# A stack of four graph layers: both score steps of the attention in a row on four banks, new step orders, and another opening

## The reference

```
layer 0: e = leaky((x W1)(x W2)^T), masked by adj; relu(softmax(e) (x W3))
layer 1: h = x W; e_ij = leaky(h_i a1 + h_j a2), masked; elu(softmax(e) h)
layer 2: o1 = relu(x mlp1 + b1)                       (512 hidden channels)
         o2 = elu(elu(GAT without a mask (W_fc, a_fc) of o1)) + o1
         o3 = relu(o2 mlp2 + b2)
         relu(elu(GAT masked by adj (W_hand, a_hand) of o3) + o3)
layer 3: attention with 4 heads of 64 channels: q, k, v with biases,
         softmax(q k^T / 8, masked) v, then wo and bo
```

## Time and profile before

| | |
|---|---|
| median of 3 runs | 2618.84 us (2617.55 to 2623.7) |
| the profiled execution | 2616.98 us, span 2615.2 us |
| mean granted TensorE clock | 0.988 |
| TensorE busy | 2525.4 us, 97% of the span, 21399 products |
| VectorE busy | 2251.1 us, 86% |
| ScalarE busy | 1968.4 us, 75% |
| GpSimd busy | 1913.2 us, 73% |
| bytes moved by DMA | 329.67 MB, 126 GB/s |

### The profile page before, as it was taken

How to read it: one execution, slowest core, us unless ns; L and a number is a source line. 1 busy time by engine, 2 the same in 40 slices (tenths; PEclk the granted TensorE clock), 3 DMA queues, 4 the chain that set the end, 5 groups by cost and what they waited for, 6 DMA issues and landing times. The chain is left out here.

```text
span 2615.2 us, 64667 instructions
## 1 busy us (share of the span) xinstructions
PE 2525.4 (97%) x21399; PEld 2411.0 (92%) x21399; DVE 2251.1 (86%) x6252; ACT 1968.4 (75%) x4737; POOL 1913.2 (73%) x2439
## 2 busy tenths in 40 slices
PE   6899999999999999999999999999999999999886
PEld 5789999999999999999999999999999999999874
DVE  2478999899999998999999999999989999998874
ACT  2468877887887788778778877877887788787652
POOL 2457877877787877778787777878777787877543
PEclk8899999999999999999999999999999999999998
DMA  4214444444444444444444444344444444443333
GB/s 141 67 52 128 129 142 130 126 139 130 136 123 145 127 126 142 129 138 121 145 126 130 139 134 133 124 142 128 131 134 136 132 128 141 128 132 110 105 106 89
DMA packets 317115, 329.67 MB, mean 126 GB/s; under 512 B 35313, under 2 KB 248689, under 8 KB 316785
## 3 DMA queue, kind: packets, MB, share of 16 engines
q1 hardware_dynamic: 316784, 325.54, 41.5%
HBM read 174.41 MB, written 150.99 MB: 124 GB/s over the span
## 5 line engine op out<-in xcount | busy, mean ns | idle before, releaser
L1234 POOL TENSOR_TENSOR p<-p,rd 128x512 f32<-128x512 f32 x256 | 343.1, 1350 | 5.5
L1159 POOL TENSOR_TENSOR proT_lo<-sco,proT_hi 128x512 fp32r<-128x512 f32 x128 | 165.8, 1295 | 159.7 <-ACT proT_hi L560 159.7
L1171 POOL TENSOR_SCALAR xn<-act,nmean,rstd 128x256 f32<-128x256 f32 x384 | 237.1, 627 | 47.7 <-DVE act L1075 35.3
L786 ACT ACTIVATE p<-p,nmx 128x256 f32<-128x256 f32 x512 | 253.0, 496 | 10.9 <-DVE nmx L1109 10.9
L573 ACT ACTIVATE sco<-sco,nmax 128x256 f32<-128x256 f32 x384 | 192.6, 502 | 40.9 <-DVE nmax L872 36.1
L1181 POOL TENSOR_TENSOR act<-act,x 128x512 f32<-128x512 f32 x64 | 82.9, 1295 | 167.8 <-ACT act L623 167.8
L1109 DVE CUSTOM_DVE_ANT_0 p<-ps,mask 128x256 f32<-128x256 f32 x512 | 188.3, 414 | 15.4 <-PE ps L510 14.0
L872 DVE CUSTOM_DVE_ANT_0 sco<-ps,mask 128x256 f32<-128x256 f32 x384 | 144.9, 414 | 53.2 <-ACT ps L563 41.2
L808 DVE TENSOR_TENSOR xnT_lo<-ps,xnT_hi 128x512 fp32r<-128x512 f32 x192 | 129.7, 675 | 61.0 <-ACT xnT_hi L560 61.0
L1166 POOL TENSOR_TENSOR rstd<-vare,mhalf 128x2 f32<-128x2 f32 x256 | 178.1, 696 | 0.0
L1124 DVE STREAM_TRANSPOSE p<-p 128x1024 f32<-128x1024 f32 x128 | 158.6, 1239 | 18.0 <-POOL p L1234 17.7
(11 more groups left out here) (240 smaller groups left out, 12396.6 us busy)
## 6 DMA issues: line engine op xcount, KB each, us to landing
scratch<-p SPq DMA_DIRECT2D x128, 512.0 KB, 3.0
p4T<-scratch SPq DMA_DIRECT2D x512, 128.0 KB, 3.5
scratch_pro<-act SPq DMA_DIRECT2D x192, 256.0 KB, 2.3
sco<-scratch_pro SPq DMA_DIRECT2D x768, 64.0 KB, 1.9
x0Tp<-in_xT SPq DMA_DIRECT2D x64, 256.0 KB, 2.6
x<-in_x SPq DMA_DIRECT2D x64, 256.0 KB, 2.8
scratch_o<-sco SPq DMA_DIRECT2D x64, 256.0 KB, 2.1
o3r<-scratch_o SPq DMA_DIRECT2D x256, 64.0 KB, 2.5
```

The costliest lines, as they stand in the source:

```text
L786: ins = nc.scalar.activation(rows_, rows_, ACT.Exp, scale=-1.0, bias=nmx4[:, h, m:m + 1], accum_out=den4[:, h, m:m + 1])
L1159: return G.tensor_tensor(lo, whole, hi.bitcast(fp32), ALU.subtract)
L1171: ins = G.tensor_scalar(xn[:, m, :], y[:, m, :], nmean[i][:, m:m + 1], rstd[i][:, m:m + 1], ALU.add, ALU.mult)
L1234: G.tensor_tensor(rows_, rows_, rd4[:, h, :].unsqueeze(2).unsqueeze(3).broadcast_to([P, NT, QUADS, CT * QP]), ALU.mult).then_inc(S["p4n"], 1)
```

## The change

- **Scores.** s40 keeps banks 7 and 6, s42 goes to banks 0 and 1 (`SCORE_BANKS`). On TensorE s40 and s42 follow each other directly, and v2 and w2 come behind them instead of between.
- **Orders.** All five lists are new. Most engines keep the sequence in the main and start the list at another place (which raises or lowers a stage by one for the steps that pass the seam). Besides the scores: on TensorE x0 moves from beside f3 to just ahead of s40, and f1 behind h0; on ScalarE g0 and a few others move, and t0 stands ahead of n2 where t1 stood; on VectorE e0 and t0 come earlier, k4 and v4 later; on GpSimd n4 follows v4 directly and k4 closes the list; on SyncE o5 follows o1, with i1 behind both.
- **Opening.** W3 and adj have a semaphore of their own (`loaded4`). A0 needs only W1T and W2T, VectorE copies and splits A0 first, then splits W3, then makes the mask. The eight loads of the last layer's weights are issued behind the load of element 1's x transposed, no longer right away. GpSimd fills the tile `ones2` at the start.
- **Spare products.** They are now products of 128 columns of ones with ones. 100 stand ahead of A0's products, 24 behind them, and 373 in front of the same 15 steps of the opening that had 95. The 52 after the opening and the 188 of the closing are gone.

```diff
@@ ORDERS @@
-    "sp": "o42:8 i40:8 i42:8 lt:0 st:9 o1:3 i1:3 o5:6 o0:1 lx:1 i0:1 o3:6 i3:6 o40:7 i5:6",
-    "pe": "x0:2 d2:5 v4:7 n2:4 s40:7 w2:5 v2:5 s42:7 a1:3 h1:2 c2:4 g0:0 a0:1 a3:6 f1:2 r2:4 h0:0 m3:5 s0:0 x1:3 f2:4 a4:7 x3:6 m2:3 y4:7 h3:5 q4:6 k4:6 f3:5",
-    "ac": "g0:1 z2:6 a3:7 b3:7 a0:2 r2:5 u1:3 h0:1 m3:6 o3:6 s0:1 x1:4 p1:3 a4:8 x3:7 f2:5 p0:1 w2:5 x2:5 h3:6 m2:4 q4:7 l0:0 u3:6 k4:7 p3:6 t1:3 n2:4 o2:4 p40:7 x0:2 t0:1 p41:7 y2:5 p42:7 t3:6 h1:2 p43:7 a1:3 k2:5 c2:4",
-    "dv": "v2:5 p41:7 s42:7 s43:7 i2:5 n2:5 p42:7 h1:2 x40:7 p43:7 b1:3 i3:6 a1:3 j2:5 c2:4 g0:0 x42:7 c3:6 z2:5 b3:6 a3:6 st1:3 ag1:3 r3:6 h0:0 z3:6 st3:6 r2:4 ag3:6 st0:1 ag0:1 e1:2 o3:5 x1:3 f2:4 t1:2 a4:7 x3:6 e0:0 b2:4 y4:7 st4:7 h3:5 t0:0 ag4:7 q4:6 e3:5 k4:6 v4:6 i0:0 d2:4 q2:4 t3:5 s40:6 rb2:4 s41:6 x0:1 p40:6 i1:2",
-    "po": "n3:7 v0:2 n4:9 m3:6 n0:2 w2:5 k4:7 l0:0 t1:3 v4:8 m2:4 d40:7 t0:1 p40:7 d41:7 p41:7 t3:6 d42:7 d43:7 p42:7 p43:7 y1:3 a0:1 v1:3 n1:3 v3:6",
+    "sp": "o0:2 i1:4 i0:2 i5:7 o3:7 i3:7 o40:8 lx:2 o42:8 st:9 i40:8 i42:8 o1:3 o5:6 lt:0",
+    "pe": "k4:7 f3:6 d2:5 v4:7 n2:4 x0:2 s40:7 s42:7 v2:5 w2:5 a1:3 h1:2 c2:4 g0:0 a0:1 a3:6 r2:4 h0:0 f1:2 m3:5 s0:0 x1:3 f2:4 a4:7 x3:6 m2:3 y4:7 h3:5 q4:6",
+    "ac": "z2:6 a3:7 b3:7 a0:2 h0:1 u1:3 r2:5 m3:6 o3:6 s0:1 x1:4 p1:3 a4:8 p0:1 x3:7 f2:5 m2:4 w2:5 x2:5 h3:6 l0:0 q4:7 t1:3 u3:6 k4:7 p3:6 t0:1 n2:4 o2:4 x0:2 p40:7 p41:7 p42:7 a1:3 y2:5 p43:7 h1:2 t3:6 c2:4 k2:5 g0:0",
+    "dv": "x40:7 i3:6 b1:3 i2:5 p43:7 n2:5 h1:2 a1:3 c2:4 j2:5 x42:7 g0:0 c3:6 z2:5 b3:6 a3:6 st1:3 r3:6 ag1:3 z3:6 h0:0 st3:6 st0:1 ag3:6 r2:4 ag0:1 e1:2 o3:5 x1:3 e0:0 t1:2 f2:4 a4:7 t0:0 x3:6 b2:4 y4:7 st4:7 h3:5 ag4:7 q4:6 e3:5 i1:2 d2:4 k4:6 v4:6 t3:5 s40:6 s41:6 s42:6 p40:6 s43:6 p41:6 q2:4 rb2:4 x0:1 p42:6 v2:4 i0:0",
+    "po": "w2:5 l0:0 t1:3 v4:8 n4:8 t0:1 m2:4 d40:7 p40:7 d41:7 d42:7 p41:7 p42:7 t3:6 d43:7 p43:7 y1:3 a0:1 v1:3 n1:3 v3:6 v0:1 n3:6 n0:1 m3:5 k4:7",
@@ spare products @@
-SPARE_OPENING = "h0:0:4 s0:0:3 g0:1:17 a0:0:7 h0:1:4 s0:1:4 x0:0:4 h1:0:15 h0:2:3 s0:2:3 x0:1:4 h0:3:3 s0:3:3 m2:0:16 a1:1:5"
-SPARE_FILLING = "r2:0:5 s0:4:3 m2:1:2 d2:0:11 m2:2:2 f3:0:29"
-SPARE_CLOSING = "m3:-5:2 x1:-3:2 ... a4:-2:25 s40:-1:1 s42:-1:5 a4:-1:52 y4:-1:5"
+SPARE_LOADING = 100
+SPARE_OPENING = "h0:0:18 s0:0:18 g0:1:57 a0:0:25 h0:1:18 s0:1:16 x0:0:18 h1:0:46 h0:2:14 s0:2:16 x0:1:18 h0:3:14 s0:3:16 m2:0:52 a1:1:27"
+            def busy(b, count):
+                for _ in range(count):
+                    nc.tensor.matmul(ps[:, b, 0:P], ones2[:, :], ones2[:, :], start=True, stop=True)
+            pe.wait_ge(S["setup_pool"], 2)
+            busy(4, SPARE_LOADING)
             pe.wait_ge(S["loaded0"], 16 * n_loads[0])
...
+            busy(4, 24)
             pe.wait_ge(S["made"], 1)
@@ loads @@
-        LOADS = (("W1T", "W2T", "W3"), ...
+        LOADS = (("W1T", "W2T"), ...
             def later_weights():
-                sp.dma_start(adj_sb, adj).then_inc(S["loaded0"], 16)
+                sp.dma_start(W["W3"], weights["W3"]).then_inc(S["loaded4"], 16)
+                sp.dma_start(adj_sb, adj).then_inc(S["loaded4"], 16)
...
-                load_weights(3)
...
                 if t == 0:
                     later_weights()
+                if t == 1:
+                    load_weights(3)
@@ scores @@
+    SCORE_BANKS = (7, 6, 0, 1)
-                            ins = nc.tensor.matmul(bank[7 - g % 2][:, m, :], qT[a][rows_, ...
+                            ins = nc.tensor.matmul(bank[SCORE_BANKS[g]][:, m, :], qT[a][rows_, ...
             def s42(t):
...
-                enter(6, "nmx4", HEADS * t + 4)
-                enter(7, "nmx4", HEADS * t + 4)
+                enter(SCORE_BANKS[2], "nmx4", HEADS * t + 4)
+                enter(SCORE_BANKS[3], "nmx4", HEADS * t + 4)
@@ layer 0: the waits go through enter() @@
             def g0(t):
                 pe.wait_ge(S["x0Tl"], t + 1)
-                wait(pe, S["nmax0"], t)
+                enter(0, "g0", t + 1)
             def h0_(t):
-                pe.wait_ge(S["g0"], t + 1)
+                pe.wait_ge(S["x0Tl"], t + 1)
+                enter(0, "h0", t + 1)
             def s0(t):
-                pe.wait_ge(S["h0"], t + 1)
+                pe.wait_ge(S["g0"], t + 1)
+                enter(0, "nmax0", t + 1)
@@ VectorE's set-up @@
-            dv.wait_ge(S["loaded0"], 16 * n_loads[0])
-            V.tensor_scalar(mask16[:, :, :], adj_sb, 0.0, MASK, ALU.is_le, ALU.mult)
-            split([whole_weight("W3")])
             dv.wait_ge(S["setup_pe"], 1)
             V.tensor_copy(A0f[:, :, :], bank[0]).then_inc(S["setup_dve"], 1)
             dv.wait_ge(S["setup_dve"], 1)
             split([(A0, slice(0, CT), slice(0, C), A0f[:, :, :])]).then_inc(S["made"], 1)
+            dv.wait_ge(S["loaded4"], 32)
+            split([whole_weight("W3")]).then_inc(S["made"], 1)
+            V.tensor_scalar(mask16[:, :, :], adj_sb, 0.0, MASK, ALU.is_le, ALU.mult)
```

More of the change, by code:

```diff
@@ L8, with spare_products @@
 ORDERS = {
[5 rows of a table removed]
-}
-SPARE_OPENING = "h0:0:4 s0:0:3 g0:1:17 a0:0:7 h0:1:4 s0:1:4 x0:0:4 h1:0:15 h0:2:3 s0:2:3 x0:1:4 h0:3:3 s0:3:3 m2:0:16 a1:1:5"
-SPARE_FILLING = "r2:0:5 s0:4:3 m2:1:2 d2:0:11 m2:2:2 f3:0:29"
-SPARE_CLOSING = "m3:-5:2 x1:-3:2 a3:-5:2 m3:-4:2 x1:-2:2 a3:-4:11 x1:-1:2 r2:-1:6 m3:-2:7 s40:-3:3 a3:-2:17 m3:-1:17 s40:-2:3 s42:-2:5 a3:-1:19 a4:-2:25 s40:-1:1 s42:-1:5 a4:-1:52 y4:-1:5"
-def spare_products(B):
[5 rows of a table added]
+}
+SPARE_LOADING = 100
+SPARE_OPENING = "h0:0:18 s0:0:18 g0:1:57 a0:0:25 h0:1:18 s0:1:16 x0:0:18 h1:0:46 h0:2:14 s0:2:16 x0:1:18 h0:3:14 s0:3:16 m2:0:52 a1:1:27"
+def spare_products():
     table = {}
-    for text, first, b in ((SPARE_OPENING, 0, 4), (SPARE_FILLING, 0, 6), (SPARE_CLOSING, B, 0)):
-        for name, t, count in (x.split(":") for x in text.split()):
-            table[name, first + int(t)] = b, int(count)
+    for name, t, count in (x.split(":") for x in SPARE_OPENING.split()):
+        table[name, int(t)] = 4, int(count)
     return table
@@ L1155, in _ @@
             G.memset(ones[:, :], 1.0).then_inc(S["setup_pool"], 1)
-            po.wait_ge(S["setup_pool"], 1)
+            G.memset(ones2[:, :].bitcast(fp32), 1.0).then_inc(S["setup_pool"], 1)
+            po.wait_ge(S["setup_pool"], 2)
             def low_part(lo, whole, hi):
```

26 lines of the change are left out of this document (11 added, 15 removed).

## The result

The kernel after takes 2654.73 us (median of 4 runs, 2651.68 to 2656.58) against 2618.2 us for the kernel before on the same chip (2616.78 to 2623.7): a ratio of 1.0138, 95% interval 1.0120 to 1.0155. It is 1.4% slower; the forecast was 2597 us, 0.8% faster, with 2617 as the upper end of its range. The profiled span is 2654.8 us against 2615.2, 39.6 us more.

A forecast was written before the change was run, and what follows sets the result against it. TensorE was taken to bound the middle, at 38.05 us a round. 2617.0 - 21.5 (middle) - 4.5 (opening) + 4 (closing) = 2595, and 1.9 for the median over the profiled run gave 2597 us; 8-in-10 range 2579 to 2617.

The forecast's parts named there:

- Rival 2: Opening: spare products cost 0.11 us each, g0 comes 5 us later, total 2609 us; chance 0.13.
- rival 4: Whole kernel: all 13.5 us of clock gained and new orders shorten the ramps by 5, total 2581 us; chance 0.16.
- The 9 us of clock: Opening: spare products raise the clock; of 13.5 us that full clock would save, 9 are put on the path.
- Nothing gained here, bounds -2.5 and +6: Start of the opening: g0 at 13.3 us instead of 13.48, despite A0 waiting for W1T and W2T alone.
- The joined scores: Middle, TensorE: s40 and s42 in a row save one visit's dear steps, 0.40 us a round.
- the stall term: Middle: waits from the closer steps cost 0.04 us a round, bounds 0 and 0.4.
- (a): Middle: n2 follows f3 0.44 us sooner; its margin on bank 1, read by the third masking, falls to about 0.
- (b): Middle: s40 needs bank 6 emptied by v4's bias add, which ends 0.05 us after s40 could start.
- (c): Middle: s42 enters bank 1 after ScalarE's read of n2's result; margin 0.25 us, of which (a) takes 0.1.
- rival 1: Middle: ring f3, u3, e3, k4, v4, s40 keeps the period at 38, total 2617 us; chance 0.12.
- Rival 3: Middle, ScalarE: t0's late return ahead of n2 holds up s42, total 2635 us; chance 0.07.
- The closing: End: +6 us for lost clock, about 1 us gained in each of the last two rounds; +4, bounds -4 and +15.

The follow-up runs named there:

- c4: Kernel after with each of the 497 spare products 256 columns wide instead of 128: 2641.84 us, ratio 1.0080 to the kernel before.
- d4: a2 with every engine's first steps (140 on TensorE, until about 275 us) in the old orders, the rest in the new: 2625.42 us, ratio 1.0029.
- a2: Kernel after, no spare products around A0 or at the end, and the old fill of 95 and 52 products of 256 columns: 2632.38 us, ratio 1.0070.
- b1: a2 with the five old orders (four score banks, early A0, s40 and s42 apart): 2669.63 us, ratio 1.0203.
- a1: Kernel after without the 100 spare products ahead of A0's and the 24 behind: 2634.24 us, ratio 1.0066.
- c2: a2 with the last layer's weight loads issued with the other weights again: 2632.09 us, ratio 1.0049.
- d2: a2 with x0 ahead of n2 on TensorE, so nothing stands between n2 and the scores: 2647.1 us, ratio 1.0110.
- f1: a2 with x0 back beside f3 and s42 in banks 3 and 0, bank 3 free once head 2 is masked: 2626.78 us, ratio 1.0026.
- d3: Kernel before without its 188 closing spare products: 2620.4 us, ratio 1.0006.

## Why the prediction was wrong

**The price of a spare product: the step that failed first.** The prediction took 0.055 and 0.107, and 0.11 and 0.213 as upper bound; measured are 0.109 and 0.213, the upper bound at both clocks. The argument was that a plain fp32 product goes through the array twice, so that an f32r one costs half of its 0.213. For wide products that is so: A0's plain fp32 products of 256 columns take 0.426 each at half clock (22.99 to 25.55 for six), the f32r ones 0.213. For narrow ones it is not. The product of two columns and the one of 128 cost the same, and so nearly does one of 256 (0.119 in c4); what all of them have in common is one loading of 128 columns of weights. The 0.09 that the prediction read for a transpose was a mean of three at 0.108 and a last one at 0.028, whose remainder lies in d2's dear first product. Rival 2's price was right. The Trainium skill ("TensorE: Matmul & The Clock Gate", section "LDWEIGHTS") gives 0.107, which the rows at full clock confirm; at half clock the rows show twice that.

**The hundred loading products.** The prediction let them end at 9.3, in the middle between the two clocks. They ended at 22.46, since the clock did not rise on them at all. It took for granted that they would raise it half way; with 256 columns, in c4, the price did fall, after the first 23. Even rival 2 (2609 us in all) had assumed a clock that rises. Its sum was also too small by its own prices: halfway between 0.11 and 0.213 the hundred end at 17.3, 8 us later and not 5, and the 18.5 beside it adds the dearer products to a 9.3 that was itself halfway between two clocks. Here the forecast was off by 15.8 us at g0 (29.12 for 13.3), and the 497 products cost 24.0 us against the old fill by the fourth d2. A part of that is the 24 behind A0's products: they last 3.5 us, longer than the 2.3 of A0's copy and split that they were to cover.

**The ramp of the new orders: not in the sum at all.** The prediction costed the orders by their middle and wrote "nothing" or a gain of 5 (rival 4) for the ramps. d4 against a2 gives 13.1 us, b1 against a2 10.6. A likely reason is that in the ramp, where most stages hold no element, a round is as long as its longest chain of waits, and that this chain changed with the order; no run shows it, and which single step of the new orders makes it so was not tried.

**The rest of the opening.** A0 is indeed ready early (g0 at 9.67 in a1), and nothing came of it (b1). The late weights cost nothing (c2) instead of 1.5. The 9 us of clock are not there: the mean clock stayed at 0.8, and the 373 products cost 6.9 us more than the 147 old ones (a1 against a2). "Nothing gained here, bounds -2.5 and +6" was too narrow, and so were the bounds of the whole opening, -14 and +12, for 36.4.

**The joined scores: right.** By medians over the rounds, from the start of one product to the start of the next: the scores take 1.626 instead of 0.915 + 0.908; v2 and w2 2.924 instead of 3.001 and a1 1.433 instead of 1.530, as one seam behind the scores goes each time. That is 0.37 of the 0.40 forecast.

**What took it back: the stall term, 0.24 where 0.04 stood.** From f3 to the first score the round got 0.25 longer. Product by product (medians over the rounds) this is not x0's move, for which the prediction took 0: f3's last product loses 0.08, n2's last loses its seam of 0.09, and x0's last transpose, now ahead of the scores, gains 0.17. That is 0 in sum, for the reason that the prediction gave. What costs is that v4 and n2 now start just when their bank comes free. The product ahead of v4 takes 0.05 more, which is the wait itself; v4's and n2's first products take 0.19 instead of 0.12; and the products behind them run at 0.117 instead of 0.113. (a) was right that n2's margin falls to about 0, but a margin of 0 is not free. v4 was overlooked: it follows q4 in bank 6, had 0.53 to spare, comes 0.44 sooner for the same reason as n2, and meets qT_lo. (b) did not bite: v4's bias add ends 0.39 ahead of s40, since x0 and these waits stand between. (c) had the margin of s42 on bank 1 positive by 0.25 with x0 in between; without x0, d2 measured -0.38. f1 gives x0 its old place, frees s42 of bank 1, and has both starts at their old price: 37.71 to 37.77 in most rounds, 0.13 to 0.19 lower. So it was the two banks that v4 and n2 meet when x0 no longer stands ahead of them, not rival 1's ring of 37.9 for the round as a whole.

**The jitter: the right mechanism at the wrong step.** Rival 3 looked at t0 ahead of n2; t0's data was in time. It was t1, moved ahead of u3 by the same edit, whose reads come late in about every fourth round. The mean of the 56 rounds is 0.14 above their median, 8 us in all, against 0.03 or 2 us before; this is what took back the 6 us that the shorter median round was worth. The forecast's gain of 1 us from o5's place is not to be seen: of 56 rounds 15 are above the median by over 0.15, against 6.

**The closing: the number is right, in part by luck.** +4 forecast, +3.6 from the sixtieth d2 on. Of its two parts, +6 for the clock and -2 for banks 6 and 7, d3 shows 0.7 to 3.6 for the spare products that held the clock, too little for the +6; the second part no run shows by itself.
